# Tail phase of a two-layer block: the written orders of work of four queues replaced by others

## The reference

```python
def _L0_ffn_ref(x, Wc, bc, W1, b1, W2, b2):      # 32 experts x 4 sets, each picks one token of 32
    ...
    result = jnp.einsum('bnesd,bntes->bntd', result_permuted, perm)
def _mlstm_head(q, k, v, ig, fg):                # 8 heads of 64
    ...
    D = jnp.exp(log_D - max_log_D)
    qk = q @ (k.T / jnp.sqrt(jnp.asarray(DH, q.dtype)))
    C = qk * D
    normalizer = jnp.maximum(jnp.abs(C.sum(-1, keepdims=True)), jnp.exp(-max_log_D))
    return C / (normalizer + EPS) @ v
...
x = x + _L1_xattn_ref(_layernorm(x, axis=-1), ctx_1024, ctx_1024, ...)
x = x + _L1_ffn_ref(_layernorm(x, axis=-1), L1_ffn_W1, L1_ffn_b1, L1_ffn_W2, L1_ffn_b2)
```

## The kernel before, in words

| job | engine | what it does |
|---|---|---|
| SC t | TensorE L1919, L1922 | scatters the experts' results (tile `res`, 1 MB for each t) back to 128 tokens |
| ADD t | VectorE L1705, L1685 | adds SC t to `x`, statistics of the norm |
| LN 0, LN 1 | ScalarE L1565 | applies the norm ahead of the heads, ahead of the FFN |
| XT, XTC | TensorE L1903, ScalarE L1583 | turns the tokens, copies them out |
| G, LOGS, ROWS, COLS, LATER | L1941 to L1943, L1594, L1716, L1956, L1744, L1600 | the gates |
| MASK p, DEC p | GpSimd L1464, L1466, ScalarE L1533 | decay matrix of head pair p, from `negm`, a load of 256 KB for each head |
| KS p, XG p | GpSimd L1476, L1488 | scaled keys, scaled tokens (`gbc` load) of pair p |
| SCO p, PROD p | TensorE L1967, VectorE L1756 | scores of pair p, times the decay |
| ST p, STATE p | TensorE L1978, VectorE L1770 | states of pair p |
| MIX p, POUT p | TensorE L1989, L1995, ScalarE L1541 | scores and states times values, copied out |
| SQ, NORM, HROOT, SCALE, ADDH, X3 | L1552, L1786, L1449, L1807, L1494, L1685 | norm of the heads, added to `x`, statistics |
| RT, XQ, CTOK, TOKENS | L1571, L1903, L1615, L1818 | tokens rounded, turned and copied for the FFN |
| UP t, EXPAND t, GELU t | L2017, L1836, L1620 | first linear layer of 128 tokens |
| HSCALE t, RH t, HT t, CH t | L1846, L1624, L1903, L1633 | hidden values rounded, turned, copied |
| DN t, FINISH t | L2033, L1857 | second linear layer, added to `x` |
| ROOT, ADDB, SHIFT, FLOOR | L1449, L1500, L1698, L1606 | small steps of the norms, bias, floor |

## Time and profile before

### The profile page before, as it was taken

One profiled execution on the slowest core, in us unless ns is written; L12 is line 12 of the kernel. 1 busy time (PEld: TensorE's weight loads), 2 busy tenths in 40 slices (PEclk: granted clock), 3 DMA queues, 4 the chain that ended last, 5 costly groups with the idle time before them and its releaser, 6 DMA issues. The chain is left out here.

```text
span 2112.0 us, 38558 instructions
## 1 busy us (share of the span) xinstructions
PE 1813.1 (86%) x13826; PEld 1098.9 (52%) x13826; DVE 1349.7 (64%) x2609; ACT 1246.3 (59%) x2373; POOL 606.0 (29%) x1107
## 2 busy tenths in 40 slices
...
GB/s 225 149 116 81 176 95 147 124 102 165 90 166 121 139 161 89 114 122 115 114 51 174 172 317 416 256 269 92 200 124 102 196 101 145 175 46 171 76 16 26
DMA packets 170811, 302.80 MB, mean 143 GB/s; under 512 B 30208, under 2 KB 77888, under 8 KB 162304
## 3 DMA queue, kind: packets, MB, share of 16 engines
...
## 5 line engine op out<-in xcount | busy, mean ns | idle before, releaser
L570 DVE TENSOR_REDUCE a_negmax<-a_score 128x1 f32<-128x512 f32 x512 | 346.9, 684 | 111.8 <-PE a_score L709 104.5
L453 ACT ACTIVATE a_prob<-a_score,a_negmax 128x512 f32<-128x512 f32 x512 | 354.2, 694 | 85.8 <-DVE a_negmax L570 84.9
L330 POOL DMA_DIRECT2D a_q_stack<-a_q_parts x512 | 251.9, 500 | 532.4 <-DVE a_q_parts L564 260.1
L709 PE MATMUL a_score<-a_k_stack,a_q_stack 128*128 128x512 f32 x512 | 357.1, 698 | 14.1 <-ACT a_prob L453 12.5
L717 PEld LDWEIGHTS a_turn<-a_ident,a_prob 128*128 128x128 f32 x2048 | 253.5, 141 | 137.2 <-issue 95.8
L717 PE MATMUL a_turn<-a_ident,a_prob 128*128 128x128 f32 x2048 | 309.0, 274 | 3.6 <-ACT a_perm L429 1.9
L338 DVE COPY a_probT<-a_turn 128x512 f32<-128x512 f32 x256 | 176.3, 689 | 201.3 <-PE a_turn L717 201.0
L338 ACT COPY a_probT<-a_turn 128x512 f32<-128x512 f32 x256 | 150.2, 587 | 248.2 <-PE a_turn L717 247.3
L709 PEld LDWEIGHTS a_score<-a_k_stack,a_q_stack 128*128 128x128 f32 x512 | 97.2, 190 | 130.5 <-issue 81.4
L2017 PE MATMUL c_ff<-c_w1T,c_xqT 128*128 128x512 bf16 x512 | 124.2, 399 | 27.1 <-DVE c_hid L1836 11.7
L791 PE MATMUL a_work<-a_cT,a_Wk 128*128 128x512 f32 x256 | 132.2, 611 | 10.0 <-DMA a_Wk<-in_L_xattn_Wk 10.0
...
## 6 DMA issues: line engine op xcount, KB each, us to landing
a_k_stack<-a_k_parts SPq DMA_DIRECT2D x512, 64.0 KB, 2.5
a_q_stack<-a_q_parts POOLq DMA_DIRECT2D x512, 64.0 KB, 2.3
scratch_res<-b_chosen SPq DMA_DIRECT2D x32, 1024.0 KB, 11.1
...
```

Source lines behind the costliest of these rows:

```text
L330: eng.dma_start(stack[kind][i * DH0:(i + 1) * DH0, M % 2, g, :].bitcast(F32), parts[kind][g * DH0:(g + 1) * DH0, part, :].bitcast(F32)).th ...
L453: nc.scalar.activation(prob[:, U % 4, :], score.bank(U)[:, :], ACT.Exp, bias=negmax[:, u:u + 1], accum_out=sums[:, head_of(U), tile_of(U): ...
L570: nc.vector.tensor_reduce(negmax[:, U % UNITS:U % UNITS + 1], score.bank(U)[:, :], AX.X, ALU.max, negate=True).then_inc(max_ready, 1)
L709: nc.tensor.matmul(score.bank(U)[:, :], stack["Q"][:, M % 2, g, t * P:(t + 1) * P], stack["K"][:, M % 2, g, :], start=True, stop=True).the ...
```

## The change

The lists of four queues are replaced; `SP_ORDER`, all functions and all sizes stay. Each job occurs as often as before. Shown are the first part of TensorE's list and the period parts of all four lists; the last parts follow the period parts in the same manner, and the first parts of the other lists change so as to fit them.

```diff
-    PE_ORDER = ((("SC", 0, 0), ("SC", 1, 0), ("SC", 2, 0), ("SC", 3, 0), ("SC", 0, 1), ("SC", 1, 1), ("XT", 0, 0),
-                 ("G", 0, 0), ("ROWS", 0, 0), ("SCO", 0, 0)),
-                (("ST", 0, -1), ("UP", 0, -2), ("UP", 1, -2), ("SCO", 1, -1), ("SC", 2, 0), ("SC", 3, 0),
-                 ("ST", 1, -1), ("MIX", 0, -1), ("ST", 2, -1), ("SCO", 2, -1), ("MIX", 1, -1),
-                 ("UP", 2, -2), ("ST", 3, -1), ("SCO", 3, -1), ("MIX", 2, -1), ("HT", 0, -2),
-                 ("MIX", 3, -1), ("SC", 0, 1), ("SC", 1, 1), ("UP", 3, -2), ("DN", 0, -2),
+    PE_ORDER = ((("SC", 0, 0), ("SC", 1, 0), ("SC", 2, 0), ("SC", 3, 0), ("SC", 0, 1), ("XT", 0, 0), ("G", 0, 0),
+                 ("ROWS", 0, 0), ("SC", 1, 1), ("SCO", 0, 0)),
+                (("XQ", 0, -2), ("ST", 0, -1), ("UP", 0, -2), ("UP", 1, -2), ("ST", 1, -1), ("SC", 2, 0),
+                 ("SCO", 1, -1), ("MIX", 0, -1), ("UP", 2, -2), ("SC", 3, 0), ("HT", 0, -2),
+                 ("SCO", 2, -1), ("ST", 2, -1), ("MIX", 1, -1), ("ST", 3, -1), ("SCO", 3, -1),
+                 ("MIX", 2, -1), ("MIX", 3, -1), ("SC", 0, 1), ("UP", 3, -2), ("DN", 0, -2),
                  ("XT", 0, 0), ("HT", 1, -2), ("G", 0, 0), ("DN", 1, -2), ("HT", 2, -2),
-                 ("HT", 3, -2), ("DN", 2, -2), ("ROWS", 0, 0), ("SCO", 0, 0), ("DN", 3, -2),
-                 ("XQ", 0, -1)),
...
+                 ("DN", 2, -2), ("SC", 1, 1), ("HT", 3, -2), ("ROWS", 0, 0), ("SCO", 0, 0),
+                 ("DN", 3, -2)),
...
-                 (("STATE", 0, 0), ("PROD", 0, 0), ("EXPAND", 0, -1), ("EXPAND", 1, -1), ("ADD", 0, 1),
-                  ("ADD", 1, 1), ("ADD", 2, 1), ("ADD", 3, 1), ("PROD", 1, 0), ("STATE", 1, 0),
-                  ("HSCALE", 0, -1), ("STATE", 2, 0), ("PROD", 2, 0), ("EXPAND", 2, -1),
-                  ("STATE", 3, 0), ("PROD", 3, 0), ("HSCALE", 1, -1), ("MOM", 0, 1), ("NORM", 0, 0),
-                  ("SHIFT", 0, 1), ("EXPAND", 3, -1), ("HSCALE", 2, -1), ("SCALE", 0, 0),
-                  ("FINISH", 0, -1), ("X3", 0, 0), ("HSCALE", 3, -1), ("FINISH", 1, -1),
-                  ("SHIFT", 1, 0), ("ROWS", 0, 1), ("TOKENS", 0, 0), ("COLS", 0, 1),
-                  ("FINISH", 2, -1), ("FINISH", 3, -1)),
...
+                 (("TOKENS", 0, -1), ("COLS", 0, 0), ("FINISH", 3, -2), ("STATE", 0, 0), ("PROD", 0, 0),
+                  ("EXPAND", 0, -1), ("ADD", 0, 1), ("EXPAND", 1, -1), ("ADD", 1, 1), ("ADD", 2, 1),
+                  ("HSCALE", 0, -1), ("STATE", 1, 0), ("EXPAND", 2, -1), ("PROD", 1, 0),
+                  ("ADD", 3, 1), ("STATE", 2, 0), ("PROD", 2, 0), ("MOM", 0, 1), ("PROD", 3, 0),
+                  ("STATE", 3, 0), ("HSCALE", 1, -1), ("SHIFT", 0, 1), ("NORM", 0, 0),
+                  ("EXPAND", 3, -1), ("HSCALE", 2, -1), ("SCALE", 0, 0), ("FINISH", 0, -1),
+                  ("X3", 0, 0), ("HSCALE", 3, -1), ("FINISH", 1, -1), ("SHIFT", 1, 0),
+                  ("ROWS", 0, 1), ("FINISH", 2, -1)),
...
-                 (("GELU", 3, -2), ("CH", 1, -2), ("RH", 2, -2), ("LOGS", 0, 0), ("RH", 3, -2), ("CH", 2, -2),
-                  ("LN", 1, -1), ("LATER", 0, 0), ("CH", 3, -2), ("RT", 0, -1), ("CTOK", 0, -1),
-                  ("DEC", 0, 0), ("DEC", 1, 0), ("GELU", 0, -1), ("FLOOR", 0, 0), ("POUT", 0, 0),
-                  ("DEC", 2, 0), ("GELU", 1, -1), ("POUT", 1, 0), ("DEC", 3, 0), ("RH", 0, -1),
-                  ("POUT", 2, 0), ("CH", 0, -1), ("POUT", 3, 0), ("SQ", 0, 0), ("GELU", 2, -1),
-                  ("LN", 0, 1), ("RH", 1, -1), ("XTC", 0, 1)),
...
+                 (("FLOOR", 0, -1), ("POUT", 1, -1), ("DEC", 3, -1), ("POUT", 2, -1), ("CH", 0, -2), ("POUT", 3, -1),
+                  ("SQ", 0, -1), ("GELU", 2, -2), ("LN", 0, 0), ("RH", 1, -2), ("XTC", 0, 0),
+                  ("GELU", 3, -2), ("CH", 1, -2), ("RH", 2, -2), ("LOGS", 0, 0), ("CH", 2, -2),
+                  ("LN", 1, -1), ("RH", 3, -2), ("LATER", 0, 0), ("CH", 3, -2), ("RT", 0, -1),
+                  ("CTOK", 0, -1), ("DEC", 0, 0), ("GELU", 0, -1), ("GELU", 1, -1), ("DEC", 1, 0),
+                  ("RH", 0, -1), ("POUT", 0, 0), ("DEC", 2, 0)),
...
-                  (("XG", 0, -1), ("MASK", 1, -1), ("KS", 2, -1), ("XG", 1, -1), ("MASK", 2, -1), ("KS", 3, -1),
-                   ("XG", 2, -1), ("MASK", 3, -1), ("XG", 3, -1), ("ADDB", 0, -2), ("ROOT", 0, 0),
-                   ("HROOT", 0, -1), ("ADDH", 0, -1), ("ROOT", 1, -1), ("KS", 0, 0),
-                   ("MASK", 0, 0), ("KS", 1, 0)),
...
+                  (("MASK", 3, -1), ("XG", 3, -1), ("ROOT", 0, 0), ("ADDB", 0, -2), ("HROOT", 0, -1),
+                   ("ADDH", 0, -1), ("ROOT", 1, -1), ("KS", 0, 0), ("MASK", 0, 0), ("KS", 1, 0),
+                   ("KS", 2, 0), ("XG", 0, 0), ("MASK", 1, 0), ("KS", 3, 0), ("MASK", 2, 0),
+                   ("XG", 1, 0), ("XG", 2, 0)),
```

More of the change, by code:

```diff
@@ L1122, in tail_phase @@
     NX, NH = 3, 3
-    PE_ORDER = ((("SC", 0, 0), ("SC", 1, 0), ("SC", 2, 0), ("SC", 3, 0), ("SC", 0, 1), ("SC", 1, 1), ("XT", 0, 0),
-                 ("G", 0, 0), ("ROWS", 0, 0), ("SCO", 0, 0)),
-                (("ST", 0, -1), ("UP", 0, -2), ("UP", 1, -2), ("SCO", 1, -1), ("SC", 2, 0), ("SC", 3, 0),
-                 ("ST", 1, -1), ("MIX", 0, -1), ("ST", 2, -1), ("SCO", 2, -1), ("MIX", 1, -1),
[6 rows of a table removed]
-                 ("ST", 1, -2), ("MIX", 0, -2), ("ST", 2, -2), ("SCO", 2, -2), ("MIX", 1, -2),
[6 rows of a table removed]
-                 ("SCO", 3, -1), ("MIX", 2, -1), ("HT", 0, -2), ("MIX", 3, -1), ("UP", 3, -2),
[4 rows of a table removed]
+    PE_ORDER = ((("SC", 0, 0), ("SC", 1, 0), ("SC", 2, 0), ("SC", 3, 0), ("SC", 0, 1), ("XT", 0, 0), ("G", 0, 0),
[3 more added lines that the diff above has]
+                 ("SCO", 2, -1), ("ST", 2, -1), ("MIX", 1, -1), ("ST", 3, -1), ("SCO", 3, -1),
[6 rows of a table added]
+                 ("HT", 0, -3), ("SCO", 2, -2), ("MIX", 1, -2), ("SCO", 3, -2), ("ST", 3, -2),
[4 rows of a table added]
+                 ("MIX", 0, -1), ("SCO", 2, -1), ("ST", 2, -1), ("MIX", 1, -1), ("UP", 2, -2),
+                 ("SCO", 3, -1), ("ST", 3, -1), ("MIX", 2, -1), ("HT", 0, -2), ("MIX", 3, -1),
[5 rows of a table added]
```

56 lines of the change are left out of this document (28 added, 28 removed), and 27 rows, old and new, of tables (ACT_ORDER, PE_ORDER).

## The result

| | before | after |
|---|---|---|
| median of 20 runs each, us | 2111.15 (2092.2 to 2128.33) | 2095.79 (2087.29 to 2104.57) |
| ratio | | 0.9936, 95% interval 0.9914 to 0.9958 |
| the profiled execution, its span | 2113.8, 2112.0 | 2093.38, 2091.5 |

The account below looks back on a forecast made before the run. It took A as bound by SC 3's res wait and slow clock, B by ScalarE; -36.6 + 4.2 + 4.2 - 1.5 = -29.7 from 2113.8, less 3.5 for the median, gave 2080.6; 8-in-10 range 2064 to 2106.

Parts of the forecast that it names:

- low level: TensorE's 1.2 GHz level: 5.3 us a period taken as gone from A, 4.2 us in all charged in B.
- what is late next: Wait at SC 2 for its res block once SC 3's wait is covered: +0.5 us a period.
- SC 3 later: SC 3 behind SCO 1, MIX 0 and UP 2: 6.7 us of cover against its 4.16 us wait for res.
- Slow stretch: TensorE's 11.9 us at the low level behind SC 3: 5.3 us of excess goes if the standstill caused it.
- HT 0 forward: HT 0 leaves its place before MIX 3, which then waits for MIX 2's copy: +0.5 us.
- A: Period's start (XQ) to the end of MIX 3: forecast 217.3 us in six periods instead of 253.9.
- Masks and XG 1: GpSimd's XG 1 behind MASK 2 ends at 24.7 us of the period, before MIX 1 needs it: cost 0.
- B: End of MIX 3 to the next XQ: +4.2 us for reordering and +4.2 for the low level, in six periods.
- First and last periods: SC 1 of batch 1 leaves the chain to the first gates: -1.5 us at the start; last batches 0.
- R1: Rival, chance 0.17: the slow stretches only move, so only the waits count: 2100 us.
- R2: Rival, chance 0.14: transfers are the bound, SC 3's wait becomes one of MASK 2 or SC 2: 2108 us.
- R3: Rival, chance 0.09: pair 3's late g load delays MIX 3 and, through ROOT 0, NORM and B: 2122 us.

Follow-up runs that it names:

- e3: The changed kernel with HT 0 back between MIX 2 and MIX 3 in the periods: 2104.01 us, 0.9970 of before.
- the second profile: The changed kernel run once more, unaltered: 2098.55 us, 0.9954 of before.
- e6: The kernel before, with stores Y 2, Y 3 and the load of x behind SC 3's res load on the SP queue: 2109.68 us, 1.0006 of before.
- e2: The changed kernel with ADDB 31 us earlier in the period on GpSimd, behind XG 0: 2084.83 us, 0.9869 of before.
- the three repairs: The changed kernel with ADD 0 behind EXPAND 1, ADDB behind XG 0 and HT 0 between MIX 2 and MIX 3: 2077.20 us, 0.9842 of before.

## Why the prediction was half right

The direction was right, and so was the source of the gain: SC 3's wait, 19.8 us in five periods, and the slow stretch behind it went. The size was not: 15.4 us came where 30 were forecast. 2095.8 misses the forecast's own range, 2066 to 2094, and lies in that of 2064 to 2106 only because this one was drawn into the rivals. Three steps failed. The low level, taken as gone with 5.3 us a period, came back at MIX 3 with 8.7 us in the six. The +0.5 for what is late next, 3 in six periods, measured 8.7. And the move of ADDB, which is in no term of the sum, made EXPAND 3 late by 7.0. Step by step:

- **SC 3 later.** The wait of 4.2 went, and so did ADD 3's. The charge of +0.5 for what is late next is the term that was mis-sized. It priced ADD 0 between EXPAND 0 and EXPAND 1 at a delay of 0.45 and looked for the DMA wait in SC 2's res block; but ADD 0 reads x too, which lands 5.6 us after its issue. UP 1 waited 0.9, 2.2, 2.0, 1.9, 2.3 and 2.0 us, UP 2 2.6 in all, together 13.9; SC 2 lost its waits of 5.2 in all. So +8.7 in six periods, some 6 more than charged.
- **Slow stretch.** It went from behind SC 3, and came back at MIX 3: 8.7 us over 2.8 in the six (2.1, 2.2, 1.5, 0.8, 0 and 2.1), after a standstill of only 0.5. *HT 0 forward* charged the 0.5 rightly, and overlooked the level that TensorE would have there. e3, with HT 0 back, shows it. These 8.7 and the 6 make 14.7 of the 16.9 by which A (234.2) missed 217.3.
- **Masks and XG 1.** XG 1 ended at 24.7 of the fourth period as said, and MIX 1 didn't wait. But both waits that were to show the forecast wrong above 2 us came. GpSimd stood for the load of MASK 2 for 2.6 to 3.9 us in five periods (3.28 in the fourth), in time that it had to spare. And XG 3 waited for g 7.4, 1.2, 2.3, 1.7 and 3.3 us in the first five periods, and 2.7 to 6.9 in the second profile. MIX 3 wasn't held by it (its 0.51 is the same in every period), but ROOT 0 was, and so ADDB.
- **B.** +8.4 forecast, +8.5 in the profile and +9.7 by the means, but in part from other causes. SC 1 was hidden, UP 3's waits grew to 2.0 in the fourth period, and DN 2 waited 2.54 and ran at the low level in five periods of six. ADDB was in no step: I had taken its move on GpSimd for free, since GpSimd has time, and didn't ask what it runs beside. The fifth period (46.6) fulfils "B over 43", and the first, second and sixth A "over 39".
- **First and last periods.** XQ 0 came 9.5 earlier in the profile, but over all profiles its mean with the first part of before is 1480.6 (four) and with that of after 1476.3 (eight): -4.3, against -1.5 forecast, within a scatter of 9 us. Counted from the tail's first SC it is 126.4 and 123.3: -3.1. The last part, put at 0, is +2.4 (121.9 and 124.4). By these means the parts are -25.5 (A), +9.7 (B), -4.3 and +2.4, together -17.7, against the 15.4 of the medians; the forecast had -36.6, +8.4, -1.5 and 0.
- **The rivals.** R1 was partly true: slow stretches moved to MIX 3, SC 0 and UP 3. R2 wasn't what happened: SC 2 didn't wait, and MASK 2's wait held up nothing of TensorE; but the x load of that chain is the new wait, and e6 shows it bind. Of R3 the first half was there, the late g and through ROOT 0 a later NORM, but only by way of ADDB: in e2 g is as late and NORM isn't.

With the three repairs the kernel runs at 2077, near the forecast of 2080, and A comes within 2.3 us of its forecast. That the totals agree so well is in part luck: B is then 252.1 where 257.7 were forecast.
